# A non-local block on one core: the last two steps written out, stores by quarters, two short runs of zero matmuls, and one split moved from GpSimd to VectorE

## What is computed

```python
q = jnp.einsum('bchw,dc->bdhw', x, theta_w) + theta_b      # d = 256
xpool = _maxpool2(x)                                       # 16 x 16 positions
k = jnp.einsum('bchw,dc->bdhw', xpool, phi_w) + phi_b
v = jnp.einsum('bchw,dc->bdhw', xpool, g_w) + g_b
qk = jnp.einsum('bdn,bdm->bnm', q, k) * hp ** (-0.5)       # 1024 x 256 per image
p = jax.nn.softmax(qk, axis=-1)
vp = jnp.einsum('bdm,bnm->bdn', v, p)
out = jnp.einsum('bdhw,cd->bchw', vp, z_w) + z_b           # back to 1024 channels
return out + x
```

## Time and profile before

| | |
|---|---|
| median of 3 runs | 2055.68 us (2054.66 to 2056.37) |
| profiled execution | 2058.26 us, span from first to last instruction 2056.5 us |
| mean granted TensorE clock | 0.996 |
| busy share of the span | TensorE 99%, VectorE 76%, GpSimd 67%, ScalarE 63% |
| DMA | 198 GB/s over the span |

### The profile page before, as it was taken

One profiled execution on the slowest core, in us unless ns is written; L12 is line 12 of the kernel. 1 busy time (PEld: TensorE's weight loads), 2 busy tenths in 40 slices (PEclk: granted clock), 3 DMA queues, 4 the chain that ended last, 5 costly groups with the idle time before them and its releaser, 6 DMA issues.

```text
span 2056.5 us, 49021 instructions
## 1 busy us (share of the span) xinstructions
PE 2033.3 (99%) x17804; PEld 2030.3 (99%) x17804; DVE 1555.1 (76%) x2623; ACT 1299.0 (63%) x2228; POOL 1369.3 (67%) x830
## 2 busy tenths in 40 slices
PE   8999999999999999999999999999999999999997
PEld 8999999999999999999999999999999999999997
DVE  7787777787777877777877778777778777787765
ACT  6667666666566666666665666666666656667653
POOL 4577666776666776677766667766777666677643
PEclk9999999999999999999999999999999999999999
DMA  7555556656556555566465665565664655665625
GB/s 231 200 188 201 198 177 216 232 172 211 175 210 225 190 197 202 175 215 237 169 211 175 208 224 194 194 205 173 215 238 170 211 175 206 224 196 192 208 103 182
DMA packets 212907, 407.27 MB, mean 198 GB/s; under 512 B 12688, under 2 KB 15760, under 8 KB 212880
## 3 DMA queue, kind: packets, MB, share of 16 engines
q1 hardware_dynamic: 212736, 406.90, 58.3%
q10 hardware_dynamic: 144, 0.01, 0.0%
HBM read 272.64 MB, written 134.22 MB: 198 GB/s over the span
## 4 chain that ended last, share of the span: by engine, by line
PE 96%; DVE 1%; DMA 1%; POOL 1%; issue 1%; ACT 0%; SPq 0%; DVEq 0%; POOLq 0%
PE bank L863 96%; DMA x<-x 1%; DVE x_top L688 0%; POOL x_split_lo L548 0%; DVE pt_raw L670 0%; DVE x_bot L688 0%; DVE pooled L642 0%; POOL att_lo L566 0%; PE bank L870 0%; ACT att_hi L392 0%; POOL att_f L561 0%; SPq L252 0%; ACT probs L453 0%; DVE xp_lo L785 0%; ACT att_f L382 0%
## 5 line engine op out<-in xcount | busy, mean ns | idle before, releaser
L548 POOL TENSOR_TENSOR x_split_lo<-x,x_split_hi 128x1024 fp32r<-128x1024 f32 x255 | 613.8, 2413 | 252.8 <-ACT x_split_hi L353 229.6
L863 PE MATMUL bank<-x_split_hi,theta_hi 128*128 128x256 f32 x2048 | 566.2, 276 | 3.0 <-DVE x_split_lo L720 2.4
L863 PE MATMUL bank<-x_split_hi,theta_lo 128*128 128x256 f32 x2048 | 566.1, 276 | 0.0
L863 PE MATMUL bank<-x_split_lo,theta_hi 128*128 128x256 f32 x2048 | 566.1, 276 | 0.0
L863 PE MATMUL bank<-att_hi,z_hi 128*128 128x256 f32 x1792 | 495.6, 277 | 6.0 <-DVE x_bot L688 3.4
L863 PE MATMUL bank<-att_hi,z_lo 128*128 128x256 f32 x1792 | 494.8, 276 | 0.0
L863 PE MATMUL bank<-att_lo,z_hi 128*128 128x256 f32 x1792 | 494.8, 276 | 0.0
L670 DVE STREAM_TRANSPOSE pt_raw<-probs 32x256 f32<-32x256 f32 x1024 | 445.8, 435 | 17.4 <-ACT probs L453 0.8
L688 DVE TENSOR_TENSOR x_top<-bank,x_top 128x512 f32<-128x512 f32 x512 | 334.8, 688 | 72.0 <-PE bank L863 67.8
L863 PEld LDWEIGHTS bank<-x_split_hi,theta_hi 128*128 128x128 f32 x2048 | 385.1, 188 | 3.5 <-issue 3.5
L566 POOL TENSOR_TENSOR att_lo<-att_f,att_hi 128x768 fp32r<-128x768 f32 x191 | 281.6, 1480 | 159.0 <-ACT att_hi L392 159.0
(11 more groups left out here) (74 smaller groups left out, 4401.5 us busy)
## 6 DMA issues: line engine op xcount, KB each, us to landing
x<-x SPq DMA_DIRECT2D x256, 512.0 KB, 3.9
x_top<-x SPq DMA_DIRECT2D x128, 512.0 KB, 7.0
x_bot<-x SPq DMA_DIRECT2D x128, 512.0 KB, 5.2
out<-x_top SPq DMA_DIRECT2D x128, 512.0 KB, 3.6
out<-x_bot SPq DMA_DIRECT2D x128, 512.0 KB, 6.6
x_top<-theta_wt SPq DMA_DIRECT2D x4, 256.0 KB, 5.8
x_top<-g_wt SPq DMA_DIRECT2D x4, 256.0 KB, 6.7
x_bot<-z_wt SPq DMA_DIRECT2D x4, 256.0 KB, 7.1
```

Of the source, the lines that this page charges most:

```text
L548: nc.gpsimd.tensor_tensor(flat(lo), flat(x_chunk(s, c)), raw(flat(hi)), ALU.subtract).then_inc(x_ready, 1)
L863: last = nc.tensor.matmul(dst, stationary(a), moving(b), start=start and n == 0, stop=stop and n == len(PRODUCTS) - 1, skip_group_check=re ...
```

## The change

In words:

- TensorE issues 24 zero matmuls ahead of the first `project_k`, and 14 behind the `project_k` of step 1, these after waiting for C11 of step 0.
- `lo_pt` of step 1 goes from GpSimd to VectorE, behind C12 of step 0.
- Step 62 (`step_last_but_one`) computes the scores of step 63 behind P5, and ScalarE and VectorE take its softmax in step 62. The transposes of step 62 begin ahead of `lo_v`. The adds are in another order.
- Step 63 (`step_last`): 36 zeros, P1, P2, P6 of step 62, `attend` of 63, then P5, P7, P3, P4 of 62 behind it, then the seven products of 63. The zeros between are gone. VectorE turns all of the probabilities at once and makes `lo_pt` of 63 itself, between A_TOP and U_TOP of step 62.
- `attend` of steps 62 and 63 writes banks 0 and 1 (`att_banks`) and does not wait for C12.
- The bottom input of step 63 is loaded in step 62 into buffers x0 and x1 (`bot_rows`, `load_last_bot`).
- The stores of step 63 go by quarters (`store_last`), in the order C11, C22, C12, C21, each when its own sum is complete.

The diff, cut:

```diff
+        def att_banks(turn, s):
+            return q_bank if is_last(turn, s) or is_last(turn, s, 1) else a_bank
+        def bot_rows(turn, s, j):
+            return xb[j][:, :, :] if is_last(turn, s) else x_bot[:, 2 * j:2 * j + 2, :]
@@ sync
+            def load_last_bot(turn, s):
+                sp.wait_ge(pooled_done, HALVES * CH)
+                sp.wait_ge(x_ready, HALVES * CH)
+                for j in range(2):
+                    sp.dma_start(bot_rows(turn, s, j), x_v[image_of(turn, s), s % 2, :, TB + 2 * j:TB + 2 * j + 2, :]).then_inc(
+                        last_loaded[j], 16)
+            def store_last(turn, s):
+                for which, rows, cols in ((C11, 0, 0), (C22, 1, 1), (C12, 0, 1), (C21, 1, 0)):
+                    at = slice(cols * HB, (cols + 1) * HB)
+                    if rows:
+                        for j in range(2):
+                            sp.wait_ge(o_added, upto(turn, s, SUMS, 2 * which + j + 1))
+                            sp.dma_start(out_v[image_of(turn, s), s % 2, :, TB + 2 * j:TB + 2 * j + 2, at],
+                                         bot_rows(turn, s, j)[:, :, at]).then_inc(bot_stored[j], 16)
+                    else:
+                        sp.wait_ge(o_added, upto(turn, s, SUMS, 2 * which + 2))
+                        sp.dma_start(out_v[image_of(turn, s), s % 2, :, :TB, at], x_top[s % 2][:, :, at]).then_inc(
+                            top_stored[s % 2], 16)
@@ step of sync
                 load_bot(turn, s - 1)
+                if is_last(turn, s, 1):
+                    load_last_bot(turn, s + 1)
@@ scalar
+            def step_last_but_one(turn, s):
...
+                hi_pt(turn, s)
+                hi_q(turn, s + 1)
+                exps(turn, s + 1)
+                normalize(turn, s + 1)
+                copy_att(turn, s)
+                hi_att(turn, s, 0)
+            def step_last(turn, s):
+                hi_att(turn, s - 1, 1)
+                hi_att(turn, s - 1, 2)
+                hi_pt(turn, s)
+                bias_bot(turn, s - 1)
+                act.wait_ge(att_ready, upto(turn, s, 3, 0))
+                copy_att(turn, s)
+                hi_att(turn, s, 0)
+                bias_top(turn, s)
+                act.wait_ge(o_done, upto(turn, s, SUMS, 0))
+                hi_att(turn, s, 1)
+                hi_att(turn, s, 2)
+                bias_bot(turn, s)
@@ gpsimd
-                lo_pt(turn, s)
+                if begun(turn, s, 2) and not is_last(turn, s):
+                    lo_pt(turn, s)
@@ vector
+            def step_last(turn, s):
+                dve.wait_ge(pt_ready, upto(turn, s, 1, 0))
+                for b in range(P // Q):
+                    transpose_probs(turn, s, b)
+                add(turn, s - 1, A_TOP)
+                lo_pt(turn, s)
+                for which in (U_TOP, C11, V_BOT, C22, C12, C21):
+                    add(turn, s - 1, which)
@@ step_odd of vector
                 add(turn, s - 1, C12)
+                if not begun(turn, s, 2):
+                    lo_pt(turn, s)
@@ tensor
+            keep_busy(o_x[1], 24)
             pe.wait_ge(w_ready, (PHI + 1) * PIECES)
             pe.wait_ge(xp_ready, 2)
             project_k()
+            def step_last_but_one(turn, s):
...
+                project_out(turn, s - 1, P6)
+                project_q(turn, s + 1, 2)
+                project_q(turn, s + 1, 3)
+                project_out(turn, s - 1, P5)
+                pe.wait_ge(o_added, upto(turn, s - 1, SUMS, 2 * C11 + 2))
+                scores(turn, s + 1)
+                project_out(turn, s - 1, P7)
+                project_out(turn, s - 1, P3)
+                project_out(turn, s - 1, P4)
+                attend(turn, s)
+            def step_last(turn, s):
+                pe.wait_ge(exp_done, upto(turn, s, NT, NT))
+                keep_busy(o_y[0], 36)
+                pe.wait_ge(o_added, upto(turn, s - 1, SUMS, 0))
+                for group in (P1, P2, P6):
+                    project_out(turn, s - 1, group)
+                attend(turn, s)
+                for group in (P5, P7, P3, P4):
+                    project_out(turn, s - 1, group)
@@ step of tensor
-                ending = not exists(turn, s, 1)
...
                     project_k()
+                    if second:
+                        pe.wait_ge(o_added, upto(turn, s - 1, SUMS, 2 * C11 + 2))
+                        keep_busy(o_y[1], 14)
                 attend(turn, s)
```

More of the change, by code:

```diff
@@ L136, in non_local_block @@
         top_loaded = [[sem(f"top_loaded{i}{j}") for j in range(2)] for i in range(2)]
+        last_loaded = [sem(f"last_loaded{j}") for j in range(2)]
         bot_loaded = [sem(f"bot_loaded{j}") for j in range(2)]
@@ L220, in upto, with is_last @@
             return turn * (PERIOD * each) + (s * each + more)
+        def is_last(turn, s, more=0):
+            return isinstance(turn, int) and PERIOD * turn + s == HALVES - 1 - more
+        def att_banks(turn, s):
+            return q_bank if is_last(turn, s) or is_last(turn, s, 1) else a_bank
+        def bot_rows(turn, s, j):
+            return xb[j][:, :, :] if is_last(turn, s) else x_bot[:, 2 * j:2 * j + 2, :]
         def image_of(turn, s, more=0):
@@ L405, in bias_bot @@
                 for j in range(2):
-                    act.wait_ge(bot_loaded[j], upto(turn, s, 16, 16))
-                    for i in (2 * j, 2 * j + 1):
-                        last = add_bias(x_bot[:, i, :], TB + i)
+                    if is_last(turn, s):
+                        act.wait_ge(last_loaded[j], 16)
+                    else:
+                        act.wait_ge(bot_loaded[j], upto(turn, s, 16, 16))
+                    for i in range(2):
+                        last = add_bias(bot_rows(turn, s, j)[:, i, :], TB + 2 * j + i)
                     last.then_inc(bot_ready, 1)
@@ L535, in _ @@
             steps(act, step)
[L536 to L539, removed]
         @block.gpsimd
@@ L686, in add @@
                         dve.wait_ge(o_added, upto(turn, s, SUMS, 2 * V_BOT + j + 1))
-                    tiles = (x_bot if rows else x_top[s % 2])[:, 2 * j:2 * j + 2, cols * HB:(cols + 1) * HB]
+                    tiles = bot_rows(turn, s, j) if rows else x_top[s % 2][:, 2 * j:2 * j + 2, :]
+                    tiles = tiles[:, :, cols * HB:(cols + 1) * HB]
                     nc.vector.tensor_tensor(tiles, source[j][:, :].rearrange("p (i n) -> p i n", n=HB), tiles,
@@ L808, in step_even, with lo_pt @@
                 add(turn, s - 1, C21)
+            def lo_pt(turn, s):
+                dve.wait_ge(pt_hi, upto(turn, s, 1, 1))
+                nc.vector.tensor_tensor(flat(pt[LO]), flat(pt_raw), raw(flat(pt[HI])), ALU.subtract).then_inc(pt_ready, 1)
+            def step_last_but_one(turn, s):
+                max_scores(turn, s)
+                invert(turn, s)
+                transpose_probs(turn, s, 0)
+                transpose_probs(turn, s, 1)
+                lo_v(image_of(turn, s))
+                transpose_probs(turn, s, 2)
+                add(turn, s - 1, A_TOP)
+                transpose_probs(turn, s, 3)
+                add(turn, s - 1, U_TOP)
+                add(turn, s - 1, C11)
+                lo_q(turn, s + 1)
+                add(turn, s - 1, V_BOT)
+                max_scores(turn, s + 1)
+                add(turn, s - 1, C22)
+                invert(turn, s + 1)
+                add(turn, s - 1, C12)
+                add(turn, s - 1, C21)
+            def step_last(turn, s):
+                dve.wait_ge(pt_ready, upto(turn, s, 1, 0))
+                for b in range(P // Q):
+                    transpose_probs(turn, s, b)
+                add(turn, s - 1, A_TOP)
+                lo_pt(turn, s)
+                for which in (U_TOP, C11, V_BOT, C22, C12, C21):
+                    add(turn, s - 1, which)
             def step_odd(turn, s):
@@ L921, in attend @@
                         for mt in range(MT):
-                            last = product(a_bank[m][:, h * HB:(h + 1) * HB], lambda a: vt[a][:, mt, m * P:(m + 1) * P],
+                            last = product(att_banks(turn, s)[m][:, h * HB:(h + 1) * HB], lambda a: vt[a][:, mt, m * P:(m + 1) * P],
                                            lambda b: pt[b][:, mt, h * HB:(h + 1) * HB], mt == 0, mt == MT - 1)
```

51 lines of the change are left out of this document (35 added, 16 removed).

## The result

The changed kernel takes 2042.58 us in the median of 5 runs (2042.11 to 2044.72), beside 2055.68 of before (2054.66 to 2056.37): ratio 0.994, 95% interval 0.9929 to 0.9952. That is 13.1 us less, where 16.7 were forecast; 2042.6 lies in the range (2036.5 to 2044), and above the forecast's own (2037 to 2041). The interval of the ratio is a gain of 9.9 to 14.6 us, so the 16.7 forecast lie outside it. The profiled execution took 2042.22 us, span 2040.4.

A forecast was written before the change was run, and what follows sets the result against it. TensorE was taken to bound the loop, so only head and tail could gain. Head 3.65 (1.5 + 2.15) plus tail 13.2 (11.1 + 2.1) made 16.8 us off 2055.68: 2039.0 us, range 2036.5 to 2044.

The forecast's parts named there:

- What bounds the kernel: From 88.17 us on the chain runs over TensorE without a break; gains lie only ahead of 88 and behind about 2000.
- Head, the 24 zeros: Ahead of the first key projection: zeros fill TensorE's 2.20 us wait at no cost and keep its clock; 1.5 us gained.
- The bound of 0: Lower bound for the 24 zeros: another engine takes up all of the gain, or the clock falls anyway.
- Head, low part and 14 zeros: At the attention of step 1: low part ready 1.0 us earlier, clock kept, scores of step 2 2.15 us earlier.
- Tail, order: Steps 62 and 63: with the work reordered, the last add ends at 2039.7, 11.1 us earlier.
- the first term: Tail: scores of 63 (2.73 us) and a 0.3 us stall ahead of attention 62 move its copy to 2010.93.
- Stores: End of the kernel: with quarter stores the span ends 3.6 us after the last add, not 5.7; 2.1 us gained.
- The sum: Whole kernel: head 3.65 plus tail 13.2 gives 16.8 us off the median of 2055.68, taken as 2039.0.
- the first rival: Clock falls in spite of the zeros, or VectorE takes up the head's first gain; 2040.5 to 2043 us, chance 0.22.
- new wait of 4 us: Tail rival: late transposes and low part, late bottom load or slow quarter stores add 4 to 8 us; chance 0.10.
- The bottom load of 62: Tail rival: ScalarE stands at this load, landing after 2043.9 against 2020.6 reckoned; time 2060 us, chance 0.01.

The follow-up runs named there:

- e1: The changed kernel without the 24 zeros ahead of the first key projection; 2043.12 us, ratio to before 0.994.
- e2: The kernel before with only the 24 zeros ahead of the first key projection; 2056.58 us, ratio to before 1.0003.
- e3: The kernel before with only the low part of step 1 on VectorE and the 14 zeros; 2052.86 us, ratio 0.9989.
- e5: The changed kernel without the 14 zeros ahead of the attention of step 1; 2042.51 us, ratio to before 0.9942.
- look 1: The kernel before, unchanged, in another single execution with its profile; 2055.64 us.
- look 2: The kernel before, unchanged, in a second further single execution with its profile; 2055.04 us.

## Why the prediction was right, and where it was off

**What bounds the kernel.** Right: from the scores of step 2 to 1996 us the chain is TensorE alone in either kernel, and only head and tail moved.

**Head, the 24 zeros: 1.5 forecast, nothing measured (e1, e2).** This step failed. "The zeros cost nothing ... 24 take 2.1 us, which fit in the 2.20 us for which TensorE stands still" took a wait of one execution for the kernel's. In the tail-only kernel it is 1.16 us and the clock holds behind it:

```profile
28.58 0.36 PE L965 MATMUL bank<-xp_hi,phi_hi 128*128 128x256 f32 x1 [1.16 <-DVE xp_lo L803]
```

In e1, e3 and both looks there is none, since TensorE itself is late, behind a fall at 14 to 18 us (0.57 to 0.62). With the wait short the zeros hold the projection back, with it long they save its clock; over the runs this comes out at nothing. The bound of 0 was the value.

**Head, low part and 14 zeros: 2.15 forecast, 2.1 without and 0.8 with the new tail.** In the profile the places are those forecast: low part done at 85.04, a wait of 0.37 us for the low keys, scores at 88.48, where about 89.0 was forecast. With the new tail the 14 zeros do nothing (e5); the move does it. But 2.15 us is right partly by luck. The mechanism that I named, the mended fall and the earlier scores, gives 1.4 to 2.0 us where the clock fell before, as in look 1, and 0.0 to 0.6 where it did not, as in look 2. Both looks have besides the slow pace that costs 2.0 us, of which I knew nothing, and which the profiled execution of before did not have.

**Tail, order: 11.1 forecast, 8.9 against an execution without a fall, 10.4 with.** Each place was met to within some tenths. With the head's 4.13 us taken off, the second copy of attention 62 was due at 2006.8 and came at 2007.4, P6 of 62 at 2013.9 and came at 2014.5, P1 of 63 at 2024.5 and came at 2025.1, the last add's end at 2035.6 and came at 2036.3. So 0.7 us were mis-sized, and 0.6 of them in the first term, the scores of 63 ahead of attention 62: from the scores of step 2 to the second copy of attention 62 pass 3.65 us more than before (2007.42 - 88.48 against 2007.90 - 92.61), where 2.73 + 0.3 were reckoned. VectorE's low part took 1.51 us, not 1.2, and was still 0.4 us early (ready at 2015.52, attention 63 starts at 2015.98). The other 1.5 us were the fall in attention 63, which was in the trace and in my sum without my seeing that it was one of chance.

**Stores: 2.1 forecast, 1.6 to 1.7 measured.** 3.6 us from the last add were forecast and are 4.1. The rate was right, 334 GB/s against the 347 of the earlier trace rows; what the sum has no term for is the time behind the last byte, 1.2 us in which nothing moves:

```profile
core 0: us, PE busy (x) PEld busy (x) DVE busy (x) ACT busy (x) POOL busy (x), PEclk, DMA share, GB/s
2036.20:2039.20 3.00, 0.00 (x0) 0.00 (x0) 0.10 (x1) 0.00 (x0) 0.00 (x0) 1.00 0.98 334
2039.20:2040.40 1.20, 0.00 (x0) 0.00 (x0) 0.00 (x0) 0.00 (x0) 0.00 (x0) 0.67 0.00 0
```

The estimate from the Trainium skill, "DMA: Bandwidth & Descriptors", "Anatomy of one DMA — SWDGE (gpsimd) path", was a landing 2.6 us after the issue. SyncE is done with issuing at 2035.73 + 1.36 = 2037.1 and the span ends at 2040.4, 3.3 us later, 0.7 us more than the estimate. The page fits its figure for one DMA on GpSimd's path; here SyncE issues, behind 0.8 MB of other stores, so this does not test it.

**The sum.** 1.5, 2.15 and 13.2 us were to come off the median. What came off is 0 for the zeros, 0.8 to 2.1 for the head's move, and 9.7 to 11.1 for tail and stores. The step that failed as a whole is "a median of 2055.68 - 16.8": a sum made against one execution, whose gains were partly the mending of its bad luck, taken from the median of others. Against its own execution it was off by 0.7 us; the other 3.0 are the 2.6 us by which that execution lay above its median and the 0.4 by which the profiled one of after lies below its own. And even the 0.7 are small by luck: the head's places moved by 4.1 us where 3.65 were forecast, partly since an input load came sooner.

**The rivals.** The result lies where the first rival stood ("the head's first gain is taken up", 2040.5 to 2043), but by neither of its mechanisms: the clock held, and it is not VectorE that takes the gain. No new wait of 4 us arose. The bottom load of 62 was late, but by less than its cover. ScalarE waited for it:

```profile
2016.84 2.62 ACT L428 ACTIVATE x_bot<-x_bot,bias 128x512 f32<-128x512 f32 x4 [2.86 <-DMA x_bot<-x]
```

I had reckoned with 2019.6, which is 2015.5 with the head's 4.13 us taken off; so it is 1.3 us late, more than the slack of 1.0 us that I gave it. GpSimd's first low part of attention 63 was ready at 2023.52 all the same, and P1 of 63 stood until 2025.09 for C21 of 62.

## What to carry to other kernels

When a profiled execution is above the median of the runs, look for stretches at the lower clock and for waits on early loads in it. Take their mending out of the sum against the median, or look at a second execution, before costing an edit meant to mend them. And filling a wait with zeros costs whatever part of it is not there in other executions; making the late operand earlier, as the move of the low part did, showed no such cost here (e5 and e3).

## What was not expected of the hardware

- TensorE starts 256-column matmuls each 0.113 or each 0.118 us at the same granted clock of 1.00. The Trainium skill, "TensorE: Matmul & The Clock Gate", "Back-to-back issue gap", gives N / 2.4 + 2.5 ns for an isolated matmul, by which 256 columns are an estimate of 109 ns, and for a stream 81 ns at 128 and 131 ns at 512 columns. It has one pace for each size, the rows have two. What sets it was not found.
- Behind waits of the same length the clock falls in some executions only. Ahead of attention 63 TensorE stood still for 2.01 us in the profiled execution of before (clock 0.79 in 2027 to 2035), and look 1 shows the same wait with 1.00 there. Of the five profiled executions with this wait of 2.01 or 2.02 us (before, both looks, e2, e3) two have the fall.
- The same split took VectorE 1.21 us at 83.83 and 1.51 us at 2014.01, while GpSimd was at its splits of the attention (2012.59 to 2016.69); at 83.83 GpSimd was idle.
